# A gated feed-forward on one core: each block's down-projection is issued two blocks behind its products instead of one

## What is computed

```python
def _layer(x, wqkv, qs, ksc, wo, lg, lb, w1, b1, w2, b2):
    ...
    x = x + o @ wo
    h = shift_token(x)
    ...
    h = (h - mu) / jnp.sqrt(var + 1e-05) * lg + lb
    h = h @ w1 + b1                      # 512 -> 2 x 1365
    a, g = jnp.split(h, 2, axis=-1)
    h = a * jax.nn.gelu(g, approximate=False)
    x = x + h @ w2 + b2                  # 1365 -> 512
    return x
for l in range(DEPTH):                   # DEPTH = 2
    x = _layer(x, ...)
```

## Time and profile before

| | |
|---|---|
| device time, median of 3 runs | 2882.83 us (2881.66 to 2883.5) |
| the profiled execution, its own time | 2882.62 us |
| its span, first to last instruction | 2880.8 us |
| PE busy | 2863.6 us (99%) |
| PE weight loads | 2521.9 us (88%) |
| DVE busy | 2069.0 us (72%) |
| ACT busy | 1346.0 us (47%) |
| POOL busy | 1308.8 us (45%) |
| bytes moved | 547.02 MB, 190 GB/s on average |

### The profile page before, as it was taken

The page is one execution under the profiler, slowest core; times in us unless marked ns, Lnnn a source line. Parts: engine busy times, 40 slices in busy tenths (PEclk is TensorE's granted clock), DMA queues, the critical chain, the costliest instruction groups (busy, mean ns, idle before and its releaser), DMA issues. The chain is left out here.

```text
span 2880.8 us, 53016 instructions
## 1 busy us (share of the span) xinstructions
PE 2863.6 (99%) x20256; PEld 2521.9 (88%) x20256; DVE 2069.0 (72%) x4135; ACT 1346.0 (47%) x2807; POOL 1308.8 (45%) x1406
## 2 busy tenths in 40 slices
PE   9999999999999999999999999999999999999999
PEld 7887888888889999999998888888888999999998
DVE  8987677776677666766657777776677776676765
ACT  7875556565564222222235566655555322223221
POOL 7857676776641211122105676776662223222221
PEclk9999999999999999999999999999999999999999
DMA  6753233322047777777783223332127777777775
GB/s 218 237 187 109 94 109 103 121 92 81 30 178 299 271 273 265 269 265 258 262 312 120 96 94 108 111 118 90 51 66 294 278 276 272 274 288 281 282 268 195
DMA packets 184897, 547.02 MB, mean 190 GB/s; under 512 B 26678, under 2 KB 82490, under 8 KB 162116
## 3 DMA queue, kind: packets, MB, share of 16 engines
q1 hardware_dynamic: 184500, 543.57, 53.0%
q10 hardware_dynamic: 144, 0.07, 0.0%
HBM read 447.11 MB, written 93.70 MB: 188 GB/s over the span
## 5 line engine op out<-in xcount | busy, mean ns | idle before, releaser
L1251 PE MATMUL quad<-fhT_f,slot_f 128*128 128x256 f32 (+1 forms) x2088 | 594.6, 285 | 0.0
L1252 PE MATMUL quad<-fhT_f,slot_f 128*128 128x256 f32 (+1 forms) x2088 | 590.0, 283 | 0.0
L1253 PE MATMUL quad<-fhT_f,slot_f 128*128 128x256 f32 (+1 forms) x2088 | 589.9, 283 | 0.0
L1253 PEld LDWEIGHTS quad<-fhT_f,slot_f 128*128 128x128 f32 (+1 forms) x2088 | 392.7, 188 | 0.0
L1252 PEld LDWEIGHTS quad<-fhT_f,slot_f 128*128 128x128 f32 (+1 forms) x2088 | 392.7, 188 | 0.0
L1251 PEld LDWEIGHTS quad<-fhT_f,slot_f 128*128 128x128 f32 (+1 forms) x2088 | 392.5, 188 | 0.0
L1674 ACT ACTIVATE gate_f_raw<-gate_f_raw,bias_f 128x512 f32<-128x512 f32 (+1 forms) x176 | 127.2, 723 | 551.1 <-DVE gate_f_raw L2097 551.1
L1542 ACT ACTIVATE lprob<-lprob,small 128x384 f32<-128x384 f32 (+2 forms) x512 | 288.7, 566 | 138.5 <-DVE small L1893 138.5
L2187 POOL TENSOR_SCALAR stats<-stats 128x1 f32<-128x1 f32 x64 | 35.4, 553 | 690.1 <-DVE stats L2037 689.3
L2304 POOL TENSOR_TENSOR turned_qk<-with_cos,with_sin 128x256 f32<-128x256 f32 x252 | 183.1, 747 | 334.3 <-DVE with_sin L1917 242.4
L1000 PE MATMUL bank_pair<-wqkv_h,hT 128*128 128x512 f32 x992 | 323.6, 407 | 0.0
(11 more groups left out here) (296 smaller groups left out, 7469.1 us busy)
## 6 DMA issues: line engine op xcount, KB each, us to landing
slot_f<-parts SPq DMA_DIRECT2D x160, 1792.0 KB, 7.5
slot_f<-parts SPq DMA_DIRECT2D x16, 1190.0 KB, 5.2
s_in<-stream SPq DMA_DIRECT2D x128, 128.0 KB, 2.8
s_res<-stream SPq DMA_DIRECT2D x64, 256.0 KB, 2.9
stream<-a_out SPq DMA_DIRECT2D x64, 256.0 KB, 2.0
res_f<-stream SPq DMA_DIRECT2D x63, 256.0 KB, 7.2
h_in_f<-stream SPq DMA_DIRECT2D x112, 128.0 KB, 6.7
parts<-part_high SPq DMA_DIRECT2D x20, 512.0 KB, 2.6
```

Source lines behind the costliest of these rows:

```text
L1251: e.matmul(bank[0:n, :], high, row_high, start=c == 0, stop=False)
L1252: e.matmul(bank[0:n, :], high, row_low, start=False, stop=False)
L1253: ins = e.matmul(bank[0:n, :], low, row_high, start=False, stop=c == 1)
```

## The change

The down-projection of a block is issued behind the products of the block two further on, at every place of both layers. The special cases at the start of a group and at the end of the last layer fall away. PE's order within a group becomes U0, D9 and U1, D10 of the group before, U2, D0, U3, D1 and so on to U10, D8. Behind the last group of the first layer D9 and D10 both follow the 24 matmuls of the next layer's projection, where before D9 stood ahead of them. In the last layer the end becomes U8, D6, U9, D7, U10, D8, D9, D10, where it was U8, D7, U9, U10, D8, D9, D10. Two of SP's waits count one down-projection less; the third (line 632) is left as it is.

```diff
         def load_attend_weights(l):
-            w.wait_ge(S("down"), GROUP * ((l * GROUPS - 1) * HC + 3))
+            w.wait_ge(S("down"), GROUP * ((l * GROUPS - 1) * HC + 2))
...
         def load_ahead(l):
-            w.wait_ge(S("down"), GROUP * ((l * GROUPS - 1) * HC + 4))
+            w.wait_ge(S("down"), GROUP * ((l * GROUPS - 1) * HC + 3))
...
                     up_third(l, g, j)
-                    if g and j == 1:
-                        down(g - 1, FULL)
-                    if j == 2:
-                        down(g, 0)
-                    last_blocks = (l, g) == (DEPTH - 1, GROUPS - 1) and j >= FULL - 1
-                    if j >= 2 and not last_blocks:
-                        down(g, j - 1)
-                    if last_blocks and j == FULL:
-                        down(g, FULL - 2)
-                        down(g, FULL - 1)
+                    if g and j < 2:
+                        down(g - 1, FULL - 1 + j)
+                    if j >= 2:
+                        down(g, j - 2)
             if l + 1 < DEPTH:
                 project(l + 1, 0, 12, 36)
+            down(GROUPS - 1, FULL - 1)
             down(GROUPS - 1, FULL)
```

## The result

The changed kernel takes **2887.25 us** (median of 20 runs, 2885.83 to 2889.9), the kernel before in the same comparison 2882.60 us (20 runs, 2881.48 to 2884.64). The ratio is 1.0016, with a 95% interval from 1.001 to 1.0022: 4.65 us or 0.16% slower, thus within the 0.2% that counts as no change here, and within the range. The sum had 2.3 us.

The account below looks back on a forecast made before the run. PE's own work was taken to bound the kernel. Terms of 0.2 - 0.5 + 1.0 + 1.6 = +2.3 us on the median of 2882.83 gave 2885.1 us, 0.08% slower, with a range of 2881.8 to 2888.3.

Parts of the forecast that it names:

- The slot waits: First group of each layer: PE waits at block 3's products for its slot to land, +1.0 and +1.6 us.
- Rival A: First groups: block 3's slot lands earlier, so PE has no wait for it; 2882.5 us, chance 0.14.
- B: Rival: block 3's slot lands much later, PE waits 10 us in the two first groups; 2892.5 us, chance 0.04.
- Between the layers: SP's loads of tables, tile and residual behind the seventh down-projection go out 5.0 us later, at no cost.
- The copied rows: Between two groups: block 10's down-projection no longer waits for its copied rows, -0.5 us, once.
- normal groups: Groups other than a layer's first: block 3's slot lands in time, U3 starts 2.74 us after U2 without a wait.
- The turns: 15 more switches from products to down-projections, at group boundaries and the last layer's end, 0.01 us each: +0.2 us.
- C: Rival: DVE becomes late at block 3 in 14 groups; 2889.3 us at 2.3 us of extra lateness, chance 0.02.
- D: Rival: the new waits drop PE's clock to 1.2 GHz for one block per layer; 2900.6 us, chance 0.01.

Follow-up runs that it names:

- tables_held: The changed kernel, with POOL's scaling of the rope tables held until DVE's 128x2048 subtraction is done: 2886.10 us, +3.34 against before.
- after_tile_early: The changed kernel, with the first groups' tile of h loaded ahead of the slot of block 2 and three down weights: 2886.60 us, +3.89 against before.
- first_new: The kernel before, with the new order in the first group of each layer only: 2885.31 us, +2.88 against before.
- first_old: The changed kernel, with the old order kept in the first group of each layer: 2884.25 us, +1.49 against before.
- slot_early: The changed kernel, with the load of block 3's slot issued ahead of SP's waits for the attention's stores: 2883.42 us, +0.66 against before.
- late_tables: The kernel before, with SP's wait ahead of the rope tables counting one down-projection more (8 for 7): 2883.92 us, +1.49 against before.
- before_again: The kernel before, unchanged, run a second time for one more trace: 2882.23 us in one run.
- before_tile_early: The kernel before, with the first groups' tile of h loaded ahead of the slot of block 2 and three down weights: 2881.74 us, -0.97 against before.
- both: The changed kernel, with block 3's slot loaded early and POOL's scaling of the rope tables held: 2883.11 us, +0.35 against before.
- all_three: The changed kernel, with block 3's slot loaded early, POOL's table scaling held and the first groups' tile of h loaded earlier: 2882.02 us, -0.41 against before.

## Why the prediction was nearly right

**The slot waits: right, in mechanism and in sum.** Forecast were 1.0 and 1.6 us, 2.6 together. With the 0.1 us in each U3, the three traces of the changed kernel have 2.60, 2.71 and 2.76 us, `tables_held` 2.83, `after_tile_early` 2.14 and `first_new` 2.95. In the changed kernel's first trace the sizes were the other way round (1.71 and 0.69). Counted from the start of U1, the slot landed after 15.7 and 13.9 us there, against 14.3 and 15.0 in the kernel before, so a landing moves by more than a microsecond from run to run; that the two layers came near the forecast together is in part luck. Rival A, no slot wait, never came in six traces (12 first groups), and B, 5 us each, neither. By medians the term may be larger: 2.88 us (`first_new`), 3.16 (changed less `first_old`), 3.99 (changed less `slot_early`). All are within what 11 runs leave open.

**Between the layers: wrong.** This is the step that failed. I took the tables' cover from PE's first use (31.7 us, then 26.6) and wrote that it "would have to vanish before this costs anything". The cover was not what counted. POOL's work on the tables moved onto DVE's 128x2048 subtraction, and PE waits for what DVE does behind that. The seven traces with late tables and POOL not held have the down-projection ahead of line 1000 at 3.45, 3.78, 3.45, 3.49, 3.72, 3.67 and 3.75 us (the three of the changed kernel, `after_tile_early`, `first_old`, `slot_early`, `late_tables`), which is 0.72 to 1.05 above 2.73, with 0.10 to 0.13 more in the projection: about 1 us where I had nothing. My rule was incomplete: of a moved transfer I followed who reads it on PE, and not which engine works on it in between and beside whom.

**The copied rows: a gain that is not of the change.** I counted 0.5 us gained by the earlier trace rows. That wait is in the first trace of the kernel before only. `before_again`, `late_tables`, `before_tile_early` and `first_new`, whose normal groups have the old order, don't have it. One row with a count of 1 was no ground for a term. The same list had a second row of the feed-forward, which I passed over: PE waited 0.2 us for ACT (`first_f`), at block 8 of the second layer.

**The turns: right.** 0.2 us were forecast for 15; the first layer alone has 0.1 to 0.2 us for its 7 and the border (681.76 in `tables_held` without its waits, 681.82 in `both`, 681.62 and 681.68 in the two traces of before). In the second layer, from the start of U1 to the start of the last down matmul less U1+U2, `both` and `before_again` agree to 0.02 us (675.71 and 675.69); these two have no wait at block 8. In `all_three`, which has it, it is 676.62.

**DVE, the clock, normal groups (C and D): right.** U3 of the sixth group starts 2.74 us behind the end of U2, with no wait, and the granted clock stays at 1.00.

**The sum again.** In place of 0.2 - 0.5 + 2.6 = 2.3 us the traces give 0.2 + 0 + 2.7 + 1.0 = 3.9 us. The measured 4.65 is twice the sum, and it lies in the range by luck: the range left room for slot waits of 5.8 us together, and something else filled it. Of the 2.35 us that were missing, 1.0 is the border, 0.5 the gain that wasn't one and 0.1 the slot. The last down matmuls of the first layer end at 1548.10, 3.8 us later than before and not 1.0. The remaining 0.75 us stays open. The three traces of the changed kernel lost 1.64 us on average to the late tile (1.64 = (0.74 + 2.33 + 1.84) / 3), the two of before 0.70, and the difference of 0.9 has about the missing size. But the layer 1 program ahead of that place is the same in both kernels, and with the tile early in both the gap is 4.86 us, so the tile doesn't explain it. The traces can't settle it either: the changed kernel's spans are 5.5 us longer on average than the two of before, and 0.6 us of this lies ahead of the first U1, where the kernels don't differ. The trace of `after_tile_early` is of the fastest of its 11 runs, 2.0 us below their median, so its waits may be smaller than usual.

## What to carry to other kernels

When a wait in a queue moves, follow each transfer behind it to every engine that touches it: what it will then run beside matters as much as who needs it last. Where a load is just in time, work that moves ahead of it waits for it (here 2.7 us in two places by the traces), and moving the load's issue ahead of unrelated waits repairs it. A wait that a trace shows once is to be seen in a second trace before it becomes a term. And where PE fills its time already, a deeper pipeline between its own stages has nothing to give: with every new wait repaired the order is as fast as the old one, by what 11 runs can tell.

## What the runs showed of the hardware

Where a DVE operation with two inputs in SBUF met one of POOL, the later one waited for the end of the first: 2.28 us became 4.48 for DVE's 128x2048 subtraction, 2.42 became 4.46 for POOL's 128x1024 product and 0.75 became 2.38 for a DVE operation on 85x512, while a DVE operation with one input in PSUM stayed at 0.67 beside POOL. The slot of block 3 (1792 KB) took 7.2 to 8.8 us where it was issued ahead of the bias and the weights (six loads in three traces), and 9.2 to 10.4 us where it was issued behind them and with the next slot following (22 loads in eleven traces). Over both feed-forwards of the changed kernel the granted clock was 1.00, with waits of PE of up to 1.54 us.
